# A graph kernel's two sorts: part of the permutation goes through indirect scatters to HBM

## The reference

```python
x = layernorm(x + arma_net(x, src, dst))        # normalized adjacency, 3 stacks
x = layernorm(x + gcn(x, src, dst))             # with loops
x = layernorm(x + rgcn(src, dst, edge_type, x)) # 9 relations, both directions, 2 layers
x = layernorm(x + sum_neighbours(x, src, dst))
```

## Time and profile before

| what | us |
|---|---|
| median of 3 runs | 4347.92 |
| lowest, highest run | 4340.5, 4348.68 |
| the profiled execution: its span | 4864.0 |
| first permutation, from the first compare to the last matmul's end | 50.2 to 269.0 |
| second permutation | 327.1 to 554.0 |

### The profile page before, as it was taken

The page is one execution under the profiler, slowest core; times in us unless marked ns, Lnnn a source line. Parts: engine busy times, 40 slices in busy tenths (PEclk is TensorE's granted clock), DMA queues, the critical chain, the costliest instruction groups (busy, mean ns, idle before and its releaser), DMA issues. The chain is left out here.

```text
span 4864.0 us, 55522 instructions
## 1 busy us (share of the span) xinstructions
PE 3316.3 (68%) x16061; PEld 2560.9 (53%) x16062; DVE 2277.9 (47%) x3880; ACT 1443.0 (30%) x2832; POOL 1744.4 (36%) x1969
## 2 busy tenths in 40 slices
PE   6979775999997999897465555555764443333359
PEld 3545423689995969783254444444632333322257
DVE  8979996244545525564343333333434222221134
ACT  5848576456666636540000000000000000000005
POOL 0000012011110102016356656666064666666631
PEclk8989898999998999997655555565776656655569
DMA  3000056388884839555311111111053111111115
GB/s 140 0 1 0 7 200 219 143 272 291 290 291 151 293 139 310 176 199 208 126 40 46 46 39 44 46 46 45 30 178 117 47 46 46 47 46 48 47 44 189
DMA packets 161511, 570.70 MB, mean 117 GB/s; under 512 B 46177, under 2 KB 54722, under 8 KB 160909
## 3 DMA queue, kind: packets, MB, share of 16 engines
q1 hardware_dynamic: 89494, 394.83, 23.5%
q0 software_dynamic: 71408, 172.45, 11.9%
q10 hardware_dynamic: 390, 0.60, 0.0%
HBM read 405.06 MB, written 162.66 MB: 117 GB/s over the span
## 5 line engine op out<-in xcount | busy, mean ns | idle before, releaser
L2027 PE MATMUL ps_sum_rgcn<-gathered_rgcn,select_sum_rgcn 128*128 x3328 | 980.0, 426 | 649.2 <-issue 624.8
L2027 PEld LDWEIGHTS ps_sum_rgcn<-gathered_rgcn,select_sum_rgcn 128*128 128x128 f32 x3328 | 752.4, 294 | 732.3 <-issue 729.7
L1943 POOL DMA_INDIRECT gathered_rgcn<-by_dst,row x782 | 737.7, 943 | 405.3 <-issue 217.5
L1609 PE MATMUL ps_sum_arma<-pair_counts_f_sum_arma,parts_sum_arma 128*128 128x448 f32 (+1 forms) x3850 | 852.0, 373 | 13.6 <-ACT pair_counts_f_sum_arma L1650 13.6
L1609 PEld LDWEIGHTS ps_sum_arma<-pair_counts_f_sum_arma,parts_sum_arma 128*128 128x128 f32 x3850 | 708.1, 190 | 67.6 <-issue 14.2
L1943 POOL DMA_INDIRECT gathered_rgcn<-by_src,row x558 | 526.4, 943 | 393.0 <-issue 152.4
L2064 ACT COPY acc_rgcn<-ps_sum_rgcn 128x128 f32<-128x128 f32 x100 | 26.5, 265 | 2060.5 <-PE ps_sum_rgcn L2027 971.3
L2101 DVE TENSOR_TENSOR select_sum_rgcn<-one_hot_sum_rgcn,ps_coef_sum_rgcn 128x2048 f32<-128x2048 bf16 x52 | 118.9, 2287 | 755.1 <-PE ps_sum_rgcn L2027 391.8
L1488 POOL DMA_DIRECT2D rows<-parts_sum_arma x275 | 153.6, 559 | 882.6 <-DVE parts_sum_arma L1697 840.2
L1959 PE MATMUL ps_got_sum_rgcn<-factor_parts,turned_sum_rgcn 128*128 x832 | 181.9, 221 | 311.4 <-DVE turned_sum_rgcn L2078 241.8
L2078 DVE COPY turned_sum_rgcn<-ps_turn_sum_rgcn 128x1024 bf16<-128x1024 bf16 x104 | 71.7, 690 | 653.1 <-DMA params_norm_h<-in_L_gnn_beta 410.0
(11 more groups left out here) (459 smaller groups left out, 5173.7 us busy)
## 6 DMA issues: line engine op xcount, KB each, us to landing
blocks_arma_mid<-pairs SPq DMA_DIRECT2D x125, 800.0 KB, 6.3
axT_arma<-pairs SPq DMA_DIRECT2D x100, 800.0 KB, 5.7
pair_counts_arma_sum<-pairs SPq DMA_DIRECT2D x50, 800.0 KB
rows<-parts_sum_arma POOLq DMA_DIRECT2D x275, 128.0 KB, 5.4
by_src<-rows_rgcn_tables SPq DMA_DIRECT2D x50, 576.0 KB
by_dst<-rows_rgcn_tables SPq DMA_DIRECT2D x50, 576.0 KB
exact<-whole_pairs SPq DMA_DIRECT2D x25, 800.0 KB, 3.3
pairs<-whole_pairs POOLq DMA_DIRECT2D x25, 800.0 KB, 5.2
```

The lines of the kernel that those rows point to most:

```text
L1609: last = nc.tensor.matmul(ps[:, g, 0:here.stop - here.start], half(part), counts[:, n % 2, here].bitcast(F32R), start=t == 0 and part == 0 ...
L1943: nc.gpsimd.indirect_dma_start(got[:, n % PLACES, :], None, table, bass.IndirectOffsetOnAxis(ap=o.row[:, n % C:n % C + 1], axis=0)).then_i ...
L2027: nc.tensor.matmul(ps[:, bass.ds(slot, P)], select[:, parity, u, :], rows[:, bass.ds(place, D)], start=False, stop=False, skip_group_check ...
```

## The change

Of each sixteen columns TensorE now permutes the codes of only 12 (even turns) or 10 (odd turns). Columns 12 to 15 or 10 to 15 go by another way: GpSimd issues for each column one indirect DMA that writes 128 pairs (high, low), 8 bytes each, to the rows slot x 416 + chunk of a table in HBM. That makes 124 scatters in the first sort and 130 in the second. SP zeroes the tables while the kernel loads, waits in the permute stage for all scatters, and reads the table back into SBUF (128 partitions x 832 f32); the end stage adds it to the PSUM sums. Empty slots go to spare rows behind the table.

VectorE compares fewer columns for `place` and `chunk`, all sixteen for `local` and `group`, and multiplies nothing; ScalarE forms high and low of the 12 or 10 columns; TensorE drops two of three matmuls for the other columns. The ranking step computes the row numbers `k.to_row`, and the code numbers lie interleaved in `k.record`.

```diff
+BY_PE = (12, 10)
+ROOM = P * C
+WAYS = 4
...
# load_stage, SP, behind the loads of x:
+            sp.wait_ge(blanked, 1)
+            for rows in k.scattered_rows:
+                sp.dma_start(rows[0:ROOM, :].rearrange("(p r c) a -> p r (c a)", p=P, r=QUARTERS),
+                             k.zeros[:, None, :].to_broadcast([P, QUARTERS, 2 * Q4])).then_inc(k.blank, 16)
# load_stage, GpSimd: a memset of k.zeros, two iotas of 128x416, a memset of k.record
...
# rank_stage, end; key 1 one instruction more, key 0 four
+                nc.vector.scalar_tensor_tensor(k.to_row[e, 0:W], ints[e, 1, :], float(C), ints[e, 2, :], ALU.mult, ALU.add)
...
+                then(nc.vector.scalar_tensor_tensor(best[e, 0, :], ints[e, 1, :], float(C), ints[e, 2, :], ALU.mult, ALU.add))
+                then(nc.vector.tensor_tensor(best[e, 1, :], best[e, 0, :], k.spare_row[e, :], ALU.subtract))
+                then(nc.vector.tensor_tensor(best[e, 0, :], best[e, 1, :], filled[e, :], ALU.mult))
+                nc.vector.tensor_tensor(k.to_row[e, :], best[e, 0, :], k.spare_row[e, :], ALU.add)
...
# Permute.run_stage, VectorE
-                    compare(self.place, o.slot_in, P).then_inc(self.placed, 1)
-                    compare(self.chunk, o.chunk_in, C)
-                    compare(self.local, o.local_in, P)
-                    dve.wait_ge(self.placed, i + 1)
-                    nc.vector.tensor_tensor(self.high[e, parity, 0:self.WEIGHED // 2, :, :],
-                                            self.place[e, parity, 0:self.WEIGHED // 2, :, :],
-                                            columns(o.high_in, P, self.WEIGHED), ALU.mult)
-                    compare(self.group, o.group_in, self.G).then_inc(self.made, 1)
+                    compare(self.place, o.slot_in, P, few).then_inc(self.placed, 1)
+                    compare(self.chunk, o.chunk_in, C, few)
+                    compare(self.local, o.local_in, P, U)
+                    compare(self.group, o.group_in, self.G, U).then_inc(self.made, 1)
# ScalarE
-                    for u in range(U):
+                    for u in range(BY_PE[parity]):
                         place = self.place[e, parity, u // 2, :, u % 2]
-                        if u >= self.WEIGHED:
-                            nc.scalar.activation(self.high[e, parity, u // 2, :, u % 2], place, ACT.Copy,
-                                                 scale=o.high_scale[e, bass.ds(i * U + u, 1)])
+                        nc.scalar.activation(self.high[e, parity, u // 2, :, u % 2], place, ACT.Copy,
+                                             scale=o.high[e, bass.ds(i * U + u, 1)])
...
# new: GpSimd and SP in the permute stage
+            rows = k.scattered_rows[1 - o.key]
+            @block.gpsimd
+            def _(gp):
+                gp.wait_ge(k.blank, 32)
+                for m, n in enumerate(self.scattered()):
+                    nc.gpsimd.indirect_dma_start(
+                        rows, bass.IndirectOffsetOnAxis(ap=k.to_row[:, n:n + 1], axis=0), k.record[:, n, :], None
+                        ).then_inc(k.scattered[m % WAYS], 16)
+            @block.sync
+            def _(sp):
+                for way in range(WAYS):
+                    k.scatters[way] += len(self.scattered()[way::WAYS])
+                    sp.wait_ge(k.scattered[way], 16 * k.scatters[way])
+                sp.dma_start(self.back[:, :, :].rearrange("p c a -> p (c a)"),
+                             rows[0:ROOM, :].rearrange("(p c) a -> p (c a)", p=P)).then_inc(self.returned, 16)
+                sp.wait_ge(self.returned, 16)
# end_stage, VectorE
-                nc.vector.tensor_copy(digits[:, 0, :], ps[:, 0, 0:C])
-                nc.vector.tensor_copy(digits[:, 1, :], ps[:, 1, 0:C]).then_inc(copied, 1)
+                dve.wait_ge(self.returned, 16)
+                for n in (0, 1):
+                    last_sum = nc.vector.tensor_tensor(digits[:, n, :], ps[:, n, 0:C], self.back[:, :, n], ALU.add)
+                last_sum.then_inc(copied, 1)
```

More of the change, by code:

```diff
@@ L406 @@
 class Permute:
-    WEIGHED = U // 2
+    PAIR = sum(BY_PE)
     G = NT * R
@@ L421, in __init__ @@
         self.chunk, self.place, self.high, self.low, self.local, self.group = (
-            c.sb(f"{name}_one_hot", [P, 2, U // 2, w, 2], FP16)
-            for name, w in (("chunk", C), ("place", P), ("high", P), ("low", P), ("local", P), ("group", self.G)))
+            c.sb(f"{name}_one_hot", [P, 2, n // 2, w, 2], FP16)
+            for name, n, w in (("chunk", BY_PE[0], C), ("place", BY_PE[0], P), ("high", BY_PE[0], P), ("low", BY_PE[0], P),
+                               ("local", U, P), ("group", U, self.G)))
+        self.back = c.sb("scattered_back", [P, C, 2])
+        (self.returned,) = c.sems("returned")
         self.placed, self.made, self.weighted, self.moved = c.sems("placed", "made", "weighted", "moved")
@@ L430, in turns, with scattered @@
             for parity in (0, 1):
-                turn(i * 2 + parity, parity)
+                turn(i, parity)
         if rest:
-            turn(whole * 2, 0)
+            turn(whole, 0)
+    def scattered(self):
+        return [n for n in range(self.columns) if n % U >= BY_PE[n // U % 2]]
     def run_stage(self):
@@ L483, in _, with turn @@
             def _(pe):
-                def turn(i, parity):
-                    pe.wait_ge(self.made, i + 1)
+                def turn(pair, parity):
+                    pe.wait_ge(self.made, pair * 2 + parity + 1)
                     for u in range(U):
-                        pair, at = divmod(u, 2)
-                        chunk = self.chunk[e, parity, pair, :, at]
-                        if u >= self.WEIGHED:
-                            pe.wait_ge(self.weighted, i * U + u + 1)
-                        nc.tensor.matmul(self.ps[:, 0, 0:C], self.high[e, parity, pair, :, at], chunk, start=False,
-                                         stop=False)
-                        if u < self.WEIGHED:
-                            pe.wait_ge(self.weighted, i * U + u + 1)
-                        nc.tensor.matmul(self.ps[:, 1, 0:C], self.low[e, parity, pair, :, at], chunk, start=False,
-                                         stop=False)
-                        nc.tensor.matmul(self.ps[:, 2, 0:self.G], self.local[e, parity, pair, :, at],
-                                         self.group[e, parity, pair, :, at], start=False, stop=False).then_inc(self.moved, 1)
+                        two, at = divmod(u, 2)
+                        if u < BY_PE[parity]:
+                            chunk = self.chunk[e, parity, two, :, at]
+                            pe.wait_ge(self.weighted, pair * self.PAIR + sum(BY_PE[0:parity]) + u + 1)
+                            nc.tensor.matmul(self.ps[:, 0, 0:C], self.high[e, parity, two, :, at], chunk, start=False,
+                                             stop=False)
+                            nc.tensor.matmul(self.ps[:, 1, 0:C], self.low[e, parity, two, :, at], chunk, start=False,
+                                             stop=False)
+                        nc.tensor.matmul(self.ps[:, 2, 0:self.G], self.local[e, parity, two, :, at],
+                                         self.group[e, parity, two, :, at], start=False, stop=False).then_inc(self.moved, 1)
                 nc.tensor.sem_inc(self.moved, 2 * U)
@@ L1756, in setup @@
     k.filled = nc.alloc_semaphore("table_filled")
+    k.blank = nc.alloc_semaphore("scattered_rows_are_blank")
+    k.scattered = [nc.alloc_semaphore(f"scattered{way}") for way in range(WAYS)]
+    k.scatters = [0] * WAYS
     k.rows_kept = [nc.alloc_semaphore(f"table_rows_kept{r}") for r in range(HOLD)]
@@ L1786, in sort_stage @@
         o.chunk_at = c.sb("chunk_at", [Q4, QUARTERS])
-        o.low_in = c.sb("low_in", [P, EC if o.key else C])
-        o.high_scale = c.sb("high_scale", [P, EC if o.key else C])
-        (o.local_in, o.high_in, o.group_in, o.slot_in, o.chunk_in) = (
-            c.sb(name, [P, EC if o.key else C], FP16) for name in ("local_in", "high_in", "group_in", "slot_in", "chunk_in"))
+        o.high, o.low = (k.record[:, 0:EC if o.key else C, n] for n in (0, 1))
+        (o.local_in, o.group_in, o.slot_in, o.chunk_in) = (
+            c.sb(name, [P, EC if o.key else C], FP16) for name in ("local_in", "group_in", "slot_in", "chunk_in"))
         rank_stage(nc, k, o, by_src)
@@ L2429, in gnn_kernel @@
         k.table_rows = dram["rows"]
+        k.scattered_rows = [nc.dram_tensor(f"scattered_rows{n}", (2 * ROOM, 2), F32, kind="Internal").ap() for n in (0, 1)]
         k.dinv_row = k.wide_row
```

47 lines of the change are left out of this document (29 added, 18 removed).

## The result

The changed kernel takes 4,420.7 us (median of four runs, 4,417.5 to 4,424.7), the kernel before 4,348.3 on the same chip: a ratio of 1.0167, 95% interval 1.0152 to 1.0183, or 72 us slower. The profiled execution has a span of 4,421.6 us, and its own time is 4,422.95: span and runs agree this time.

What follows compares the result with a forecast made beforehand. VectorE was taken to bound the kernel, ScalarE after the change. With scatters left uncovered, the stages were +55.5 and +58.5 us, with small edits +117: 4,465 us. Range 4,325 to 4,540, leaving out fully hidden scatters (0.20, 4,248).

Steps and rivals of the forecast that it cites:

- the second rival: Permutations: a scatter waits only for the running compare's end, two or three pass a turn; 4,345 to 4,440 us, chance 0.32.
- VectorE bounds the kernel before, and the compares' prices: Permutations: VectorE sets the pace, 8.35 us a turn; compares cost 0.52 ns an element and 0.07 us fixed.
- ScalarE becomes the bound: Permutations after the change: ScalarE needs 13.3 us a pair of turns, against VectorE's 12.7 and TensorE's 11.4.
- its change of turns: ScalarE between turns: taken as 0.15 us, so 0.3 a pair on top of 13.0 for 44 ACTIVATEs.
- Small edits: Ranking, load and end stages: extra instructions, decodes and zeroing cost +3 us together, between 0 and +8.
- A compare with two SBUF inputs holds a scatter, which then needs 0.82 us more: GpSimd beside VectorE: inferred from two delayed gathers beside L752; whoever is first holds the other off.
- It waited out the whole run, not one instruction: Permutations: from one 3.57 us direct store; one scatter passes per pair, 112 and 117 follow uncovered; case chance 0.48.
- That this gap is the profile's: Scatters: the 0.30 us idle before each was taken as profiling only, so 0.94 us each in the median run, not 1.25.
- the 516 us of the earlier trace: Whole kernel before: profiled span exceeded the median run by 516 us, 0.33 us for each of 1,564 gathers.
- The two last steps: Permutations: one scatter a pair, leaving 112 and 117, and 0.94 us for each, giving 105 and 110 us uncovered.
- Landing and read-back: Behind the last scatter of each sort: 3.5 + 3.5 = 7 us, between 5 and 10.
- That the 8-byte writes might bind: Rival at the scatters: each microsecond beyond 0.94 a scatter adds 0.23 ms; no separate chance, counted inside the ranges.

Runs made afterwards that it cites:

- 7: Two of the 44 products of a pair of turns moved from ScalarE to VectorE, in the kernel of experiment 3; 4,275.0 us, ratio 0.9826.
- 8: TensorE's code matmuls done ahead of VectorE's `group` compare, in the kernel of experiment 3; 4,249.0 us, ratio 0.9767.
- experiment 3: Changed kernel with the step numbers, each compare's second input, in PSUM instead of SBUF; 4,264.6 us, ratio 0.9799 to the kernel before.
- experiment 5: Kernel of experiment 3 plus 36 TENSOR_SCALARs ahead of VectorE's turns and 8 direct stores in the first sort; 4,284.7 us, with 3,328-byte rows 4,285.8.
- 6: Changed kernel with compares ordered place, local, chunk, group and 6 of 32 columns of a pair scattered instead of 10; 4,307.8 us, ratio 0.9899.
- 1: Changed kernel with VectorE's compares ordered place, local, chunk, group instead of place, chunk, local, group; 4,388 us, ratio 1.0081.
- 2: Compare order of 1, with `chunk` and `group` each in two instructions of half the columns; 4,358 us, ratio 1.0011.

## Why the prediction came out as it did

The direction was right, and the time 44 us too high. What happened is the second rival at its upper bound, GpSimd between two compares at 1.25 us, priced at 4,440. Step by step:

- **VectorE bounds the kernel before, and the compares' prices**: right. `chunk` starts `local` after 2.67 and 2.24 us, `place` the next after 0.88 and 0.73, each within 0.01 of the working.
- **"ScalarE becomes the bound", 13.3 us a pair**: the number was right (13.24) and the reason wrong. ScalarE's 44 products take 12.9; the 0.3 that I added for its change of turns was in truth its wait on the loop over the buffer. Experiments 7 and 8 show it. An agreement to 0.5% proved nothing about the mechanism.
- **Small edits +3, between 0 and 8**: 5.9.
- **A compare with two SBUF inputs holds a scatter, which then needs 0.82 us more**: right to 0.03 us, and experiment 3 shows that the second SBUF input is the cause. That GpSimd, where it is first, holds VectorE off is not seen at these compares (a `chunk` of 12 columns took 2.75 us throughout); at TENSOR_SCALARs it is (experiment 5).
- **"It waited out the whole run, not one instruction", hence one scatter a pair**: this step failed. The wait ends with the running compare, gap or none; 63 and 66 were out instead of 12 and 13. The store had waited out its run (experiment 5), but I carried that wait from one kind of transfer, beside one kind of instruction, over to another pair of kinds, from one row out of 25.
- **"That this gap is the profile's", hence 0.94 instead of 1.25 a scatter**: this failed too. The train has a pitch of 1.26 in an execution whose span is its own time, so the 0.30 us are real. The gathers of the table stages have the same idle time before them in both traces; the groups of the larger of their lines, before and after (busy us, mean ns, idle us before by releaser):

```profile
L1943 POOL DMA_INDIRECT gathered_rgcn<-by_dst,row x782 | 737.7, 943 | 405.3 <-issue 217.5 <-PE ps_sum_rgcn L2027 92.2 <-remote 61.0
```

```profile
L1981 POOL DMA_INDIRECT gathered_rgcn<-by_dst,row x782 | 737.8, 944 | 238.3 <-issue 220.7 <-PE ps_sum_rgcn L2065 17.7
```

  217.5 and 220.7 us of "issue" for 782 gathers, yet the 516 us of the earlier trace rows are gone. Nearly all of them lay behind the GCN layer, which ends at 2,185.0 of 4,864.0 before and at 2,256.5 of 4,421.6 after, and in these rows it is the idle time for other things that falls, from 187.8 to 17.6; that a number divides into 0.33 per gather was chance.
- **The two last steps erred in opposite directions**: 112 scatters x 0.94 = 105 us of train were forecast, 61 x 1.26 = 77 came. That the time came so near was luck.
- **Landing and read-back 7 us**: 5.1. (The row that gave a gather's 5.2 us shows no size; 64 KB is the size of the RGCN gathers.)
- **That the 8-byte writes might bind**: they land in 2.2 us, and experiment 3 runs all 254 at a pitch of 1.26.

What would have made the change pay, as given, is to take away one of the two SBUF inputs (experiment 3), to send fewer columns (6), or to let compares end more often and at the right moments (1 and 2).

## What to carry to other kernels

Before giving an idle engine work beside a busy one, ask which operand both have to fetch over the same way, and whether the busy one can fetch it elsewhere: here one constant tile moved to PSUM was worth 156 us. A price taken from one row wants the minimum and maximum of its line beside it, and a pace that agrees with a sum of one engine's work is still to be checked against the loop through the buffers (fill, then use, then free), which no engine's busy time shows. Whether work fits beside other work is decided by how often the other lets go, so count the ends per turn against the pieces per turn.

## What the runs showed of the hardware that I had not expected

- A scatter gets in at the end of a compare even when the next one has started without a gap, and costs that one nothing: `local` takes 1.22 us beside a scatter, and 1.22 before, without one.
- A direct store of GpSimd runs at 0.53 us beside the compares that hold a scatter for up to 2.78 us, or 3.50 with a long one to sit through.
- A VectorE compare of fp16 is as fast with its second input in PSUM as in SBUF: 2.746 against 2.752 us for 4,992 elements.
- Beside TENSOR_SCALARs it went both ways: a lone direct store that came into a run of them waited, mostly for the run's end (17 of 19), up to 4.67 us; a chain of stores (0.55 us each) or scatters (0.96) that had begun first was not held.
- Consecutive scatters on GpSimd start 1.26 us apart, 0.96 busy and 0.30 idle, with nothing beside them.
